# Wide cross attention on one core: scores in 128x32 tiles, value products in pairs, another order on VectorE

## The reference

```python
def xattn(hidden, ctx, mask, Wq, Wk, Wv, Wo, q_norm_w, k_norm_w):   # hidden, ctx: 32 x 64 x 512
    q = (hidden @ Wq.T).reshape(32, 64, 32, 128).transpose(0, 2, 1, 3)
    k = (ctx @ Wk.T).reshape(32, 64, 8, 128).transpose(0, 2, 1, 3)
    v = (ctx @ Wv.T).reshape(32, 64, 8, 128).transpose(0, 2, 1, 3)
    q = rmsnorm(q) * q_norm_w
    k, v = repeat(k, 4), repeat(v, 4)             # each key and value head serves four query heads
    k = rmsnorm(k) * k_norm_w
    scores = q @ k.T / sqrt(128) + mask
    out = softmax(scores) @ v
    return out.reshape(32, 64, 4096) @ Wo.T
x = x + xattn(layernorm(x), ctx, ...)
```

## Time and profile before

| | |
|---|---|
| median of three runs | 2255.3 us |
| the profiled execution | 2255.08 us, of which span 2253.3 us |
| TensorE busy | 2185.9 us (97%), 15918 matmul records |
| TensorE's weight loads busy | 1736.1 us (77%) |
| VectorE, ScalarE, GpSimd busy | 1368.5 us (61%), 1016.5 us (45%), 886.7 us (39%) |
| granted TensorE clock, mean | 0.997 |

### The profile page before, as it was taken

One profiled execution on the slowest core, in us unless ns is written; L12 is line 12 of the kernel. 1 busy time (PEld: TensorE's weight loads), 2 busy tenths in 40 slices (PEclk: granted clock), 3 DMA queues, 4 the chain that ended last, 5 costly groups with the idle time before them and its releaser, 6 DMA issues. The chain is left out here.

```text
span 2253.3 us, 39463 instructions
## 1 busy us (share of the span) xinstructions
PE 2185.9 (97%) x15918; PEld 1736.1 (77%) x15918; DVE 1368.5 (61%) x2383; ACT 1016.5 (45%) x1734; POOL 886.7 (39%) x659
## 2 busy tenths in 40 slices
PE   6997999999999999999999999999999999999998
PEld 4775878778787787877878777888887777777776
DVE  6887534343333453334333548797795888888866
ACT  6774543445435454354543552111102666666532
POOL 2675231432414423143241345221122768777611
PEclk9999999999999999999999999999999999999999
DMA  4000111110112101111010113000002000100002
GB/s 165 2 20 21 57 39 38 38 57 19 38 38 75 57 20 38 38 38 57 20 38 36 43 59 102 1 0 0 0 1 75 20 1 28 36 26 11 2 1 75
DMA packets 23032, 80.65 MB, mean 36 GB/s; under 512 B 4048, under 2 KB 6224, under 8 KB 16720
## 3 DMA queue, kind: packets, MB, share of 16 engines
q1 hardware_dynamic: 22864, 78.28, 10.2%
HBM read 74.08 MB, written 4.19 MB: 35 GB/s over the span
## 5 line engine op out<-in xcount | busy, mean ns | idle before, releaser
L2570 PE MATMUL xat_TP<-shared_rounded 128*128 128x512 f32 x1024 | 322.6, 396 | 5.8 <-issue 5.8
L2244 POOL TENSOR_TENSOR xat_T<-xat_T,xat_mask 128x512 f32<-128x512 f32 x64 | 81.7, 1299 | 514.3 <-DVE xat_T L2334 514.3
L104 PE MATMUL xat_G<-xat_xnT_hi,shared_rounded 128*128 128x512 f32 x768 | 244.4, 391 | 0.0
L2231 POOL TENSOR_TENSOR shared_rounded<-shared_landing,shared_rounded 128x2048 fp32r<-128x2048 f32 x39 | 179.4, 4607 | 153.4 <-ACT shared_rounded L2088 153.4
L2570 PEld LDWEIGHTS xat_TP<-shared_rounded 128*128 128x128 f32 x1024 | 187.2, 188 | 58.2 <-issue 22.4
L2361 DVE TENSOR_TENSOR X<-X,xat_TP 128x512 f32<-128x512 f32 x128 | 86.9, 679 | 198.5 <-PE xat_TP L2570 198.5
L2570 PE MATMUL xat_TP<-shared_rounded,xat_oT_lo 128*128 128x512 f32 x512 | 199.9, 390 | 0.0
L2325 DVE RECIPROCAL xat_q_inv_rms<-xat_OT 128x16 f32<-128x16 f32 x32 | 8.3, 260 | 312.7 <-PE xat_OT L2497 312.7
L104 PE MATMUL ffn_H<-shared_rounded 128*128 128x448 f32 (+1 forms) x816 | 179.1, 368 | 3.2 <-DVE ffn_h_kept L1397 1.9
L1329 POOL TENSOR_TENSOR ffn_one_hot<-ffn_one_hot,ffn_block_rank 128x448 f32<-128x448 f32 x64 | 75.5, 1180 | 253.4 <-DVE ffn_one_hot L1378 253.4
L687 POOL TENSOR_TENSOR two_T<-two_T,two_row_max 128x512 f32<-128x512 f32 x128 | 131.5, 1049 | 103.2 <-DVE two_row_max L778 102.9
(11 more groups left out here) (359 smaller groups left out, 5021.7 us busy)
## 6 DMA issues: line engine op xcount, KB each, us to landing
shared_landing<-in_Cq_q SPq DMA_DIRECT2D x16, 1024.0 KB, 4.9
shared_landing<-in_Cq_o SPq DMA_DIRECT2D x16, 1024.0 KB, 4.8
shared_landing<-in_Cq_kv SPq DMA_DIRECT2D x8, 1024.0 KB, 6.9
shared_landing<-in_ctxT_paired SPq DMA_DIRECT2D x4, 1024.0 KB, 6.9
two_ctxT_raw<-in_ctxT SPq DMA_DIRECT2D x8, 512.0 KB, 3.8
shared_landing<-in_w1T SPq DMA_DIRECT2D x8, 448.0 KB, 3.8
shared_landing<-in_w SPq DMA_DIRECT2D x7, 512.0 KB, 3.6
out<-X SPq DMA_DIRECT2D x6, 512.0 KB, 3.0
```

The costliest lines, as they stand in the source:

```text
L104: last = eng.matmul(out, a, b, start=(n == 0), stop=(n == len(steps) - 1))
L2231: return eng.tensor_tensor(w[1][:, :, :], landed[:, :, :], w[0][:, :, :].bitcast(F32), ALU.subtract)
L2244: eng.tensor_tensor(T[:, n, :, :], T[:, n, :, :], mask[:, :].unsqueeze(1).to_broadcast([P, ROWS, SEQ]), ALU.add)\
L2570: last = eng.matmul(TP[m % 2][:, :], x, w, start=(n == 0), stop=(n == len(steps) - 1))
```

## The change

`scores(n)` is written with 32 matmuls of 32 stationary columns in place of 16 of 64. Four chunks c of 32 query tokens go to the four groups of 32 output partitions, with the tile position given. `values(0)` moves ahead of `scores(3)`, right behind `values(1)`; `values(2)` moves from behind `output(3)` into its middle, right behind `values(3)`. VectorE does `take_scores(2)` before `low_oT(1)`, `shift(2)` before `low_oT(0)`, `shift(3)` before `add_y(0)`, and `invert(3)` before `add_y(1)`.

```diff
@@ VectorE, in each pass
                 invert_q(1)
+                take_scores(2)
                 low_oT(1)
-                take_scores(2)
                 take_scores(3)
+                shift(2)
                 low_oT(0)
-                shift(2)
+                shift(3)
                 add_y(0)
-                shift(3)
                 invert(2)
+                invert(3)
                 add_y(1)
-                invert(3)
@@ TensorE, scores(n)
                         for h in range(NH):
-                            for b in range(2):
-                                tok = (2 * u + t) * P + b * SEQ
+                            for c in range(P // QC):
+                                b = c * QC // SEQ
+                                tok = (2 * u + t) * P + c * QC
                                 key = st * STOK + (2 * u + b) * P + t * SEQ
                                 at = (h * 2 + t) * SEQ
-                                last = eng.matmul(S[u][b * SEQ:(b + 1) * SEQ, at:at + SEQ],
-                                                  qT[:, h, tok:tok + SEQ], kT[:, gg, key:key + SEQ],
-                                                  start=True, stop=True)
+                                last = eng.matmul(S[u][c * QC:(c + 1) * QC, at:at + SEQ],
+                                                  qT[:, h, tok:tok + QC], kT[:, gg, key:key + SEQ],
+                                                  start=True, stop=True, tile_position=(0, c * QC))
@@ TensorE, output(m)
                         if m == 3 and n == len(steps) // 2:
                             values(3)
+                            values(2)
@@ TensorE, in each pass
                 turn_rms(1)
                 values(1)
+                values(0)
                 scores(3)
-                values(0)
                 eng.wait_ge(wo_lo.sem, wo_lo.at(j, 1))
...
                 output(3)
-                values(2)
```

## The result

| | before | after |
|---|---|---|
| median, 13 runs of each | 2255.2 us | 2261.5 us |
| ratio, 95% interval | | 1.0027 [1.0019, 1.0035] |
| the profiled execution | 2255.08 us, span 2253.3 | 2260.55 us, span 2258.7 |
| TensorE busy, records | 2185.9 us, 15918 | 2168.9 us, 17966 |

What follows compares the result with a forecast made beforehand. TensorE's nearly gapless records were taken as the bound. Per pass -0.35 - 0.17 - 0.24 - 0.31 + 0.87 = -0.20, over 14 passes -2.8, plus 1.5 for passes 6 and 7, gave 2254.0 us, range 2246 to 2263.

Steps and rivals of the forecast that it cites:

- First half: First sums of squares to `turn_rms`: one tile shape for sums and scores takes 2.17 in place of 2.52, -0.35 us a pass.
- second half: Later sums and scores up to `turn_rms`: one tile shape shortens both blocks, -0.17 us a pass.
- turn_rms to output(0): Values and scores before `output(0)`: fewer changes of shape, 2.97 in place of 3.21, -0.24 us a pass.
- The fourth transposes' wait: TensorE's second four transposes: GpSimd's last product comes 0.3 early in the new order, so the stall goes, -0.31 us a pass.
- values(2) into output(3): `output(4)` still starts 1.82 after `output(3)`'s last matmul, so four value rounds lengthen `output(3)` in full: +0.87 us a pass.
- the chain: End of `output(3)`, then VectorE's `add_y(3)` and `low_oT(3)`, then `output(4)`: 1.82 us from the last matmul, not shortened.
- add_y(0): VectorE's `add_y(0)` behind `shift(3)` ends at 846.8, `output(2)` wants its bank at 847.03: margin 0.1 to 0.2, costed at nothing.
- Passes 6 and 7: GpSimd's context work delays the masks, stalling `output(2)` 1.2 in pass 7: +0.5 and +1.0, together +1.5 us.
- my second rival: VectorE is late for `output(2)`: 0.3 to 0.5 us a pass, 5 to 8 in all, so 2259 to 2262; chance 0.17.

Runs made afterwards that it cites:

- `low_oT(0)` ahead: Changed kernel with `low_oT(0)` moved ahead of `shift(2)` on VectorE, nothing else: 2254.1 us, 0.9993 of the kernel before.
- Half a mask: Changed kernel with GpSimd adding the mask to only half of the rows of unit 3, VectorE's list untouched: 2255.0 us, 0.9996 of the kernel before.

## Why the prediction was wrong

The forecast's steps, in their order:

- *First half, second half, turn_rms to output(0)*: right, -0.76 forecast and -0.85 measured. `scores(0)` starts 0.05 behind ScalarE's last head (0.09 forecast), the blocks of scores take 0.92 to the same shape and 1.01 to another.
- *The fourth transposes' wait*: right in size (-0.31) and, by the runs, in cause: the order on VectorE removes it, and `values(0)` first, by itself, makes it 0.20 longer. In the changed kernel TensorE comes 0.55 later as well, which hides some of it; with `low_oT(0)` ahead TensorE comes in time (8.35) and the stall is still gone (0.76).
- *values(2) into output(3)*: right, +0.86, and its cause shown by taking the chain away.
- *add_y(0)*: **this is the step that failed.** I put its end 0.1 to 0.2 ahead of the time at which `output(2)` wants its bank and cost it at nothing. In the median of the passes it ended 0.28 behind that time (0.23 after the start of the last matmul of `output(1)`), `output(2)` started 0.43 late, and the piece grew by 0.55 a pass, about 8 in all. The term inside it that was wrong is "shift(2), 845.50 - 844.11 = 1.39". I carried that length from a place where GpSimd's mask was nearly over to one where it runs from start to end: in the new order `shift(2)` took 847.18 - 845.25 = 1.93, 0.54 more. Half a mask, and `low_oT(0)` ahead, both took it away again. A smaller thing was missing too: `output(2)` starts 0.15 behind the end of `add_y(0)`, and a late start costs 0.12 more in the stretch behind it, so the margin was all but used up before the subtract came into it. In the run with VectorE's order alone that made 0.23 of an end 0.04 ahead.
- *Passes 6 and 7*: +2.0 in place of +1.5. The stall is of the kind forecast (the context's low part, then the masks), and in pass 7 the same blocked subtract adds to it (1.05 long, 0.76 before): 1.6 in place of 1.2. No run takes the context's part out of these two passes.
- One more part was in no step: a stop of 1.1 us within a block of scores in pass 15 (the last section).

So 14 times +0.25, +2.0 and +1.2 for pass 15 make +6.7; the profiled executions differ by 5.5 and the medians by 6.3. Most of the 1.2 between 6.7 and 5.5 lies behind the last pass, where both kernels have the same code: from the last matmul of the block's outputs to the end it took 907.1 us before and 905.8 after. Over the fourteen kernels here it ranges from 905.5 to 907.5, so this is no effect of the change.

The outcome is that of my second rival, VectorE late for `output(2)`, in its place and, from 0.3 to 0.5 a pass, nearly in its price. I gave it 0.17 and held against it that "the operations' lengths hardly vary". That was false in the very trace I had. In pass 8 of the kernel before, first half, VectorE has

```profile
827.86 1.05 DVE L2341 TENSOR_TENSOR xat_T<-xat_T,xat_row_max 128x512 f32<-128x512 f32 x1
...
829.54 0.69 DVE L2341 TENSOR_TENSOR xat_T<-xat_T,xat_row_max 128x512 f32<-128x512 f32 x1
```

and GpSimd

```profile
825.82 2.55 POOL L2244 TENSOR_TENSOR xat_T<-xat_T,xat_mask 128x512 f32<-128x512 f32 x2 [46.88 <-DVE xat_T L2334]
```

The masks end at 828.37, the first subtract at 828.91. Of the 64 subtracts of the kernel before, the 32 that begin beside a mask are long (0.76 or 1.05), the 32 others take 0.69. The average of a line hides this; its timeline beside GpSimd's shows it. The old order kept `low_oT(0)` between `take_scores(3)` and `shift(2)`, and it was the cover for this lock. I had named that edit (the shifts "would run beside GpSimd's masks") and not asked what it costs.

The Trainium skill states the rule: "SBUF — State Buffer", section "Who interferes with whom", calls the ports that VectorE and GpSimd share an exclusive lock, says that a VectorE instruction with two inputs in SBUF contends with a GpSimd instruction that reads SBUF, and that a reduction, or an instruction with at most one SBUF input outside the modes that use both pairs of ports, does not. The traces agree: beside a mask the subtract (both inputs in SBUF) goes from 0.69 to 1.29, while the reduction stays at 0.68 and the two low parts, with `low_oT(0)` ahead, at 1.28. That the ports are what holds it is the page's account; the runs show that GpSimd's instruction does.

The rule that I had weighed instead, the Trainium skill's floor of about 25 ns between starts ("TensorE: Matmul & The Clock Gate", section "Wait — 56ns, not 53.3ns?"), does not hold for four tiles side by side: 64 records take 0.92 to the next block's start, 14 ns each. The prediction says that no run shows whether it holds for four tiles; that was a misreading, for in the kernel before the first four records of the earlier trace rows, one in each of four tiles, start within 20 ns.

## What to carry to other kernels

Before moving an operation on VectorE, look at what GpSimd does in the new place: an operation with both inputs in SBUF can't run beside GpSimd's own elementwise work, one that reads PSUM can, so put those beside each other. A length read in one place holds in another only if its neighbours on the other engines are the same; where a line's lengths differ in the trace, find out why before adding it into a chain. And where a margin comes out smaller than the error of the sum, price both sides of it: here a margin of 0.1 to 0.2 us stood beside a term that came out 0.54 longer. One call moved by one place was worth 7 us in one spot and 28 in another.

## What the runs showed of the hardware

- A VectorE subtract with both inputs in SBUF that begins beside a GpSimd mask ends 0.55 us after that one's end, however early it began (0.74, 0.76, 1.05 and 1.30 long in the kernels above). In the kernel before and the changed one all 64 such subtracts end 0.54 or 0.55 behind. That is less than the 0.69 that one takes alone; no run shows which part of it goes ahead.
- Four 128x32 tiles with 64 columns run side by side: within a round the records start 6 to 7 ns apart, and a round takes 56 ns, as two 128x64 tiles did (58). The forecast had 55 for it. The 0.06 that the first half gained over the forecast has two parts: 0.03, as `scores(0)` starts closer behind ScalarE, and 0.03 in the blocks behind it (2.14 in place of 2.17).
- In pass 15, TensorE stops within the second block of scores:

```profile
1304.79 0.95 PE L2516 MATMUL xat_S<-xat_kT,xat_qT 128*32 128x64 f32 x53
1306.62 0.41 PE L2516 MATMUL xat_S<-xat_kT,xat_qT 128*32 128x64 f32 x11 [0.88 <-issue]
```

  There is nothing it waits for in the code between two matmuls of one block. The stop is there in all nine kernels with narrow scores and in none of the five with wide ones. It always stands behind the 53rd record of this block in pass 15, though the block starts anywhere from 1273 to 1305 us, and takes 0.9 to 1.4 us. In each of the nine, a 16 KB packet of the DMA queue that the profile calls "instruction" ends 1.3 to 1.5 us before TensorE goes on (in the changed kernel at 1305.24, with the next matmul at 1306.62), and the narrow kernels have 137 packets on that queue where the wide ones have 121. In the changed kernel no other block of scores stops, though such packets come all through it. So the loading of the longer instruction list may be what holds it; no run tested it, and it stays open. With the narrow scores alone there are two smaller stops too, of 0.3 us, in passes 3 and 9.
- The idle time that a profile gives to "issue", or to the engine that came last by its records, was VectorE's twice here. The code's own waits and a run with `low_oT(3)` ahead of `add_y(3)` in each kernel told it apart.
